# GpSimd forms u in 16 products of four channels a group instead of 8 of eight, with the decay slots turned from group to group, a loop of six groups and a reordered start

## The chip, the cores and the metric

The kernel runs on one core of a Trainium2 chip. The metric is the device time of one execution in microseconds (us); lower is better. The engines are TensorE (PE, its weight loads PEld), VectorE (DVE), ScalarE (ACT), GpSimd (POOL) and SyncE (SP), which issues the DMAs.

## The reference

The input has 128 sequences of 375 tokens with 64 channels (the tail that the means drop is not loaded: 372 are used). Three selective-scan layers follow one another, halving the length after the first two (372, 186, 93); then a diagonal state-space mixer and a routed small network, each added to its input. One scan layer is, cut to its core:

```
A = -exp(A_log)                                  # (64 channels e, 64 states n)
dlt, Bm, Cm = split(x @ W_dbc.T)                 # 1, 64 and 64 columns
delta = softplus(dlt * W_dt + b_dt)              # (b, l, 64)
dA = exp(delta[..., None] * A)
dBx = (delta * x)[..., None] * Bm[:, :, None, :]
h_t = dA_t * h_(t-1) + dBx_t                     # along l, for each channel and state
y = einsum('blen,bln->ble', h, Cm) + D * x       # then the mean of two neighbours
```

The mixer behind it is a linear recurrence with constant complex factors (tables of sines and cosines are made for it once), the network picks one of 32 experts by an argmax.

## The kernel before, in words

Two sequences are put side by side, one state of one of the two sequences on each of the 128 partitions. A group is 744 columns' worth of tokens for two halves: 372 columns a channel. There are 64 groups in layer 0, 32 in layer 1 and 16 in layer 2, 112 in all. A group has 64 channels, taken as 32 pairs; a pair is one scan of 2 x 372 = 744 columns.

For each pair four engines work in a chain. PE spreads delta over the states (`spread_delta`, L400, two matmuls) into one of three slots of PSUM. ACT takes the exponential with the factor A in place (`decay`, L706, two activations). DVE runs the recurrence (`scan`, L923) from the decay slot and from u, into hT. PE then contracts hT with C (`fill`, L418), and ACT reads that out (`read_z`, L715). The slot of pair p is `p % 3` in every group (`pair_slot`), so a group's pairs 0 and 1 take the slots of pairs 30 and 31 of the group before: 32 isn't a multiple of three, and `spread_delta` waits there for a scan that lies two back, and three back elsewhere.

u is delta times x times B. DVE forms dx = delta * x once a group (`times_x`, L934), SP stores it to HBM, and SP loads it back, each channel broadcast over 64 partitions, in 16 pieces of two pairs, each two DMAs (`broadcast`, L294). u has four buffers of four pairs each, two pieces in one. POOL multiplies a whole buffer in place by B (`inject`, L1122): 2976 columns, once both pieces are there. DVE waits for u once in four pairs. A piece is loaded again once the scans of its two pairs are over (`s_scan`).

In between the engines prepare the next group: PE the three products with x (`item`) and the sums of the softplus (`sum_delta`, `take_off`), ACT its functions and B and C (`take_B`, `take_C`), at fixed pair numbers in each engine's `body`. PE also has matmuls whose result is thrown away (`keep_busy`, L428), three each at pairs 1, 8, 16 and 24. Every engine's instruction order is written out by hand; nothing is scheduled. `layer_bodies` writes the first two and the last two groups of a layer out and runs the others in a loop of two groups.

Ahead of the first group, all constants are loaded before the first x (L247 to L255); PE and ACT wait for all eleven. The tables of the mixer (L960 to L1005 on DVE, a chain of small operations with a handoff each; L835 to L841 on ACT with two loads of a function table) stand behind the preparation of group 0 and ahead of its first scan.

Of the kernel before, what the change touches and what calls it, by code (L numbers as in the profile page):

```python
# [11 lines left out]
P = 128  # L12
# [8 lines left out]
EPT = D // TILES_G  # L21
SLOTS = 3
# [36 lines left out]
def tower(nc, io, hs, out_dram, n_batch):  # L59
# [13 lines left out]
    with ctx:  # L73
# [47 lines left out]
        s_const, s_cast, s_dout, s_zero = sem("constants_loaded"), sem("spread_cast"), sem("d_out_ready"), sem("zeros_set")  # L121
# [8 lines left out]
        s_bc = [sem(f"broadcast{i}_loaded") for i in range(RING)]  # L130
# [72 lines left out]
        N_CONST = 11  # L203

        def pair_slot(p):

            return db[p % SLOTS][:, BANK - W0:BANK + W0]

# [5 lines left out]
        def layer_bodies(eng, body):  # L214


            def group(l, g):
                n = groups[l]
                here = (l, g)
                if isinstance(g, int) and g < 2:  # L220
                    prev = (l, g - 1) if g else ((l - 1, groups[l - 1] - 1) if l else None)
                    before = (l - 1, groups[l - 1] - 2 + g) if l else None
                else:
                    prev, before = (l, g - 1), (l, g - 2)
                if isinstance(g, int) and g == n - 1:
                    after = (l + 1, 0) if l + 1 < LAYERS else None
                else:
                    after = (l, g + 1)
                return here, prev, before, after

            for l in range(LAYERS):
                n = groups[l]
                for g in range(2):
                    body(g % 2, *group(l, g))
                with eng.Fori(1, n // 2 - 1) as k:
                    for half in range(2):
                        body(half, *group(l, 2 * k + half))
                for g in range(n - 2, n):
                    body(g % 2, *group(l, g))
# [6 lines left out]
        def _(sp):  # L246
            for dst, src in ((wdt, io["wdt"]), (wB, io["wB"]), (wC, io["wC"]), (a_log, io["a_log"])):  # L247
                sp.dma_start(dst[:, :, :], src.rearrange("l p m -> p l m")).then_inc(s_const, 16)
            sp.dma_start(cols[:, :], io["cols"]).then_inc(s_const, 16)
            sp.dma_start(d_diag[:, :, :], io["d_diag"].rearrange("l p m -> p l m")).then_inc(s_const, 16)  # L250
            sp.dma_start(own[:, :], io["own"]).then_inc(s_const, 16)
            sp.dma_start(tmap[:, :], io["tmap"]).then_inc(s_const, 16)
            sp.dma_start(eye[:, :], io["ident"]).then_inc(s_const, 16)
            for i in range(2):
                sp.dma_start(hT[i][:, 0:EPT * P // 2], io["spread"][:, i * EPT * P // 2:(i + 1) * EPT * P // 2]).then_inc(s_const, 16)  # L255

# [66 lines left out]
            def body(half, here, prev, before, after):  # L323
# [21 lines left out]
            load_x(first, 0)  # L345
            sp.dma_start(s5c, io["s5c"]).then_inc(m_small, 16)
            sp.dma_start(times, io["times"]).then_inc(m_small, 16)
            store_dx(first, 0)
# [29 lines left out]
        def _(pe):  # L378
            pe.wait_ge(s_const, 16 * N_CONST)
            pe.wait_ge(s_cast, 1)  # L380
            pe.wait_ge(s_zero, 5)
            pe.wait_ge(s_dout, 1)
            pe.wait_ge(s_neg, 2)

            def spread_delta(at, buf, p):
# [10 lines left out]
                slot = pair_slot(p).rearrange("p (e s t) -> p e s t", e=2, t=T)  # L396
# [107 lines left out]
            def body(half, here, prev, before, after):  # L504
                for p in range(PAIRS):
                    spread_delta(here, half, p)
# [6 lines left out]
                    if p in (8, 16, 24) or p == 1 and prev:  # L513
                        keep_busy(here, half, -1 if p == 1 else q - 1)
# [12 lines left out]
            item(first, 0, 0)  # L527
            for i in range(3):
                sum_delta(first, i)
            take_off(first, 0)  # L530
            take_off(first, 1)
            item(first, 0, 1)
            item(first, 0, 2)
            layer_bodies(pe, body)
# [142 lines left out]
        def _(act):  # L677
# [3 lines left out]
            act.wait_ge(s_const, 16 * N_CONST)  # L681
            nc.scalar.activation(a_log[:, :, :], a_log[:, :, :], ACT.Exp).then_inc(s_aexp, 1)
            act.wait_ge(s_aexp, 1)
            nc.scalar.mul(a_neg[:, :, :], a_log[:, :, :], -1.0).then_inc(s_aneg, 1)
            for l in range(LAYERS):
                last = nc.scalar.mul(d_diag[:, l, :], d_diag[:, l, :], 0.5 if pair_mean[l] else 1.0)
            last.then_inc(s_dout, 1)
            nc.scalar.mul(neg_eye[:, :], eye[:, :], -1.0).then_inc(s_neg, 1)  # L688
            act.wait_ge(s_aneg, 1)
            act.wait_ge(s_zero, 5)  # L690

            def decay(at, p):
                l, g = at
                T = LENGTHS[l]
                slot = pair_slot(p)
# [34 lines left out]
            def take_B(at, buf):  # L730
                n = G(at)
                act.wait_ge(s_item, 3 * n + 2)
                if not known_below(n, 2):
                    act.wait_ge(s_u, PRODS * (n - 1))
# [53 lines left out]
            def body(half, here, prev, before, after):  # L788
                for p in range(PAIRS):
                    decay(here, p)  # L790
# [37 lines left out]
            high(first)  # L828
            middle(first)
            low(first)  # L830
            take_B(first, 0)
            take_C(first, 0, 0)
            take_C(first, 0, 1)
            act.wait_ge(m_small, 16 * N_SMALL)
            nc.scalar.activation(col[:, 0:1], s5c[:, 2:3], ACT.Exp).then_inc(m_acol, 1)  # L835
            act.wait_ge(m_tab, 1)
            nc.scalar.activation(col[:, 3:4], col[:, 1:2], ACT.Exp).then_inc(m_acol, 1)
# [5 lines left out]
                act_func_set_id=EXPS_ON_JOINT_TABLE))  # L843
            layer_bodies(act, body)
# [54 lines left out]
        def _(dve):  # L899
# [7 lines left out]
            dve.wait_ge(s_const, 16 * N_CONST)  # L907
            for i in range(2):
                src = hT[i][:, 0:EPT * P // 2].rearrange("p (r m) -> p r m", m=P)
                last = nc.vector.tensor_copy(spread[:, i * EPT // 2:(i + 1) * EPT // 2, :], src)  # L910
            last.then_inc(s_cast, 1)
            dve.wait_ge(s_cast, 1)

            def scan(at, p):
# [8 lines left out]
                nc.vector.tensor_tensor_scan(hT[q % 2][:, i * PAIR:(i + 1) * PAIR], pair_slot(p),  # L923
# [12 lines left out]
            def body(half, here, prev, before, after):  # L936
                for p in range(PAIRS):
                    scan(here, p)
                    if after and p == 9:
                        times_x(after, 1 - half)  # L940

            times_x((0, 0), 0)
# [35 lines left out]
            ts(red, red, PI_LO, -PI_LO, ALU.min, ALU.max).then_inc(m_tab, 1)  # L978

# [131 lines left out]
        def _(pool):  # L1111
            tt = nc.gpsimd.tensor_tensor

            def inject(at, buf, c):

                n = G(at)
                slot = c % RING
                pool.wait_ge(s_bc[slot], 32 * HALVES * (PRODS // RING * n + c // RING + 1))
                if c == 0:
                    pool.wait_ge(s_read, 3 * n + 2)  # L1120
                here = u[slot][:, :].rearrange("p (e t) -> p e t", t=W0)
                tt(here, here, Bt[buf][:, :].unsqueeze(1).broadcast_to([P, 2 * HALVES * CHUNK, W0]), ALU.mult).then_inc(s_u, 1)  # L1122

            def body(half, here, prev, before, after):
                for c in range(PRODS):
                    inject(here, half, c)
# [139 lines left out]
```

## Time and profile before

| | |
|---|---|
| median of 3 runs | 6324.4 us (6324.39 to 6329.62) |
| the profiled execution's own time | 6317.07 us |
| its span, first to last instruction | 6315.2 us |
| busy: DVE, POOL, PE, ACT | 95%, 93%, 79%, 79% |
| DMA: mean rate, share of the 16 engines | 247 GB/s, 76% |
| TensorE clock granted, mean | 0.905 of full |

The profile comes from one execution. The span is what the trace covers. Busy shares are means over stages with different limits; a group of instructions is given with its line in the kernel, its count and the mean time of one. A wait is given with what ended it. "issue" means that nothing the profile shows was waited for. Lines of the timeline give the start, the time taken by the merged instructions and, in brackets, the idle time ahead of them.

### The profile page before, as it was taken

How to read it: one execution, taken by the hardware profiler on the slowest of the kernel's cores; microseconds unless marked ns; L12 is line 12 of the kernel's file. 1: busy time of each engine (PE TensorE's matmuls, PEld its weight loads, DVE VectorE, ACT ScalarE, POOL GpSimd, SP SyncE). 2: the span in 40 equal slices, each digit the busy share in tenths (PEclk: the TensorE clock that was granted, in tenths of full speed). 3: DMA queues.
4: the chain of work that ended last, by engine and by line, in shares of the span. 5: the costliest groups of instructions: out<-in, count | busy, mean ns of one | idle time of the engine just before them, and what ended most of it. 6: DMA issues, size and time to landing. Idle time of an engine off the chain costs nothing.

```text
span 6315.2 us, 115575 instructions
## 1 busy us (share of the span) xinstructions
PE 4964.2 (79%) x35373; PEld 2008.5 (32%) x35373; DVE 6002.6 (95%) x4016; ACT 4959.9 (79%) x10247; POOL 5895.7 (93%) x996
## 2 busy tenths in 40 slices
PE   5777777777877777777787877778777778777789
PEld 2333333333333333333333333333333333333234
DVE  7999999999999999999999999999999999999965
ACT  5888888888888888888888877787887888887744
POOL 6999999999999999999999999999999999999933
PEclk7999999999899999999989888898998898998899
DMA  6887788787888888878888877788787787887810
GB/s 196 261 261 262 260 263 260 263 260 263 259 262 260 262 262 262 262 261 261 262 261 264 261 258 254 256 260 260 256 260 252 258 263 261 266 259 260 264 41 14
DMA packets 561605, 1561.17 MB, mean 247 GB/s; under 512 B 172113, under 2 KB 320530, under 8 KB 561298
## 3 DMA queue, kind: packets, MB, share of 16 engines
q1 hardware_dynamic: 561426, 1559.30, 76.0%
q8 instruction: 49, 0.80, 0.1%
q14 instruction: 130, 1.06, 0.0%
HBM read 1468.37 MB, written 90.59 MB: 247 GB/s over the span
## 4 chain that ended last, share of the span: by engine, by line
DVE 47%; issue 27%; PE 16%; POOL 4%; ACT 3%; DVEq 1%; DMA 1%; SPq 0%; ACTq 0%; POOLq 0%
DVE hT L923 46%; PE z_bank L418 5%; POOL u L1122 4%; PE decay L400 4%; ACT decay L706 2%; PE decay L540 2%; PE z_bank L428 1%; PE prep_bank L499 1%; DVEq L922 1%; PE decay L598 1%; DVE dx L934 1%; PE prep_bank L618 1%; PE prep_bank L444 1%; DMA u<-dx_rows 1%; PE decay L604 0%
## 5 line engine op out<-in xcount | busy, mean ns | idle before, releaser
L1122 POOL TENSOR_TENSOR u<-u,Bt 128x2976 f32<-128x2976 f32 x896 | 5788.6, 6495 | 219.0 <-DMA u<-dx_rows 217.3
L923 DVE TENSOR_TENSOR_SCAN hT<-decay,u 128x744 f32<-128x744 f32 x3584 | 5767.9, 1682 | 144.5 <-ACT decay L706 141.4
L706 ACT ACTIVATE decay<-decay,a_neg 128x371 f32<-128x371 f32 (+2 forms) x7168 | 3634.8, 555 | 641.1 <-PE decay L400 615.2
L400 PE MATMUL decay<-stk,spread 96*128 96x371 bf16 (+2 forms) x7168 | 1924.1, 356 | 1301.4 <-DVE hT L923 1206.3
L418 PE MATMUL z_bank<-hT,Cst 128*32 128x256 f32 x21472 | 1630.6, 427 | 0.0
L400 PEld LDWEIGHTS decay<-stk,spread 96*128 96x128 bf16 x7168 | 452.9, 101 | 2853.8 <-DVE hT L923 2616.7
L715 ACT COPY z_sb<-z_bank 128x512 f32<-128x512 f32 x1342 | 805.6, 600 | 375.3 <-PE z_bank L418 374.6
L418 PEld LDWEIGHTS z_bank<-hT,Cst 128*32 128x32 f32 x21472 | 601.4, 118 | 787.9 <-issue 545.0
L428 PE MATMUL z_bank<-stk,spread 96*128 96x372 bf16 x1341 | 325.5, 357 | 0.0
L499 PEld LDWEIGHTS prep_bank<-tmap,yT 64*128 64x128 f32 x1344 | 203.5, 215 | 134.5 <-issue 133.2
L499 PE MATMUL prep_bank<-tmap,yT 64*128 64x32 f32 (+3 forms) x1344 | 243.2, 306 | 0.7 <-DMA yT<-y_rows 0.7
L472 PE MATMUL prep_bank<-delta,eye 128*128 128x372 f32 x448 | 182.7, 489 | 2.2 <-DVE dx L934 1.7
L428 PEld LDWEIGHTS z_bank<-stk,spread 96*128 96x128 bf16 x1341 | 143.7, 107 | 106.0 <-issue 39.1
L444 PE MATMUL prep_bank<-xT,w_dt_rows 128*128 128x372 f32 x224 | 131.1, 678 | 16.1 <-ACT neg_eye L688 13.0
L1153 POOL TENSOR_TENSOR hT<-hT 128x372 f32<-128x372 f32 x16 | 15.5, 972 | 134.5 <-DVE hT L1038 134.5
L744 ACT ACTIVATE Cst<-prep_bank,own_batch 128x384 f32<-128x384 f32 x224 | 132.3, 591 | 1.7 <-PE prep_bank L444 1.7
L866 ACT ACTIVATE hT<-decay,u 128x372 f32<-128x372 f32 x64 | 36.5, 570 | 110.4 <-PE z_bank L604 110.4
L721 ACT ACTIVATE t_abs<-prep_bank,cols 128x372 f32<-128x372 f32 x112 | 74.3, 663 | 47.0 <-issue 24.7
L454 PE MATMUL prep_bank<-t_w,eye 128*128 128x372 f32 x224 | 98.3, 522 | 1.8 <-ACT t_w L753 1.8
L768 ACT COPY delta<-prep_bank 128x372 f32<-128x372 f32 x112 | 52.5, 469 | 57.0 <-PE prep_bank L462 56.6
L474 PE MATMUL prep_bank<-parts,neg_eye 128*128 128x372 bf16 x336 | 91.3, 326 | 0.0
L461 PE MATMUL prep_bank<-t_ln,eye 128*128 128x372 f32 x224 | 89.8, 482 | 0.0
(138 smaller groups left out, 2497.8 us busy)
## 6 DMA issues: line engine op xcount, KB each, us to landing
u<-dx_rows SPq DMA_DIRECT2D x3584, 372.0 KB, 4.1
delta_parts<-parts SPq DMA_DIRECT2D x112, 279.0 KB, 6.8
stk<-delta_parts SPq DMA_DIRECT2D x112, 279.0 KB, 5.3
y_rows<-z_sb SPq DMA_DIRECT2D x1792, 12.0 KB
yT<-y_rows SPq DMA_DIRECT2D x112, 192.0 KB, 4.4
dx_rows<-dx SPq DMA_DIRECT2D x112, 186.0 KB, 2.8
xT<-in_x SPq DMA_DIRECT2D x64, 186.0 KB, 4.3
xP<-in_x SPq DMA_DIRECT2D x64, 186.0 KB, 4.1
```

What stands on the lines that cost most here:

```text
L400: nc.tensor.matmul(slot[:, e, :, 1:], spread[0:PARTS * QR, TILES_G * q + er // TILES_G, :], src[:, er % TILES_G, :, 1:], start=True, stop= ...
L418: last = nc.tensor.matmul(bank[TB * 2 * g:TB * 2 * (g + 1), kk * EPT * TB:(kk + 1) * EPT * TB], Cst[buf][:, CG * (2 * i + kk) + g, :, :], ...
L428: nc.tensor.matmul(zb[:, 0:W0], spread[0:PARTS * QR, 0, :], stk[buf][0:PARTS * QR, 0, :], start=True, stop=True)
L444: nc.tensor.matmul(prep[:, 0:W0], (wdt, wB, wC)[i][:, l, :], xT[buf][:, :], start=True, stop=True).then_inc(s_item, 1)
L472: nc.tensor.matmul(prep[:, 0:W0], eye[:, :], delta[:, :], start=True, stop=False)
L499: last = nc.tensor.matmul(prep[:, k * w:k * w + m], yT[:, k, :], tmap[:, base:base + m], start=False, stop=(k == KB - 1))
L540: return nc.tensor.matmul(dst, wt, src, start=start, stop=stop)
L706: last = nc.scalar.activation(bank, bank, ACT.Exp, scale=a_neg[:, l, c:c + 1])
L715: nc.scalar.copy(z_sb[buf][:, 2 * i:2 * i + 2, :, q * EPT:(q + 1) * EPT], src).then_inc(s_zev, 1)
L744: ins = nc.scalar.activation(Cst[buf][:, :, b, :], prep[:, 0:COLS_Z].rearrange("p (k t) -> p k t", t=TB), ACT.Identity, scale=own[:, b:b + 1])
L923: nc.vector.tensor_tensor_scan(hT[q % 2][:, i * PAIR:(i + 1) * PAIR], pair_slot(p), u[c % RING][:, part * PAIR:(part + 1) * PAIR], 0.0, AL ...
L1122: tt(here, here, Bt[buf][:, :].unsqueeze(1).broadcast_to([P, 2 * HALVES * CHUNK, W0]), ALU.mult).then_inc(s_u, 1)
```

## The change

- u: `inject` is called 16 times a group, each with one piece (two pairs, four channels, 1488 columns), and waits for that piece alone; there are eight semaphores for the pieces instead of four, and `scan` waits for u once in two pairs.
- Slots: `pair_slot(turn, p)` goes on from group to group, so that each pair waits for the scan three before it.
- Loop: since the slots come round after three groups and the two sets of buffers after two, the loop holds six groups (`ROUND_OF_GROUPS`).
- Idle-filling matmuls: `keep_busy` at pair 25 too, and `keep_busy_in_prep`, three more at pair 31.
- Start: the inputs of the tables and of the first product are loaded first and have a semaphore of their own; DVE makes the tables' first half before anything else, and ACT's functions of A follow behind the first B.

```diff
+ROUND_OF_GROUPS = 6
-        def pair_slot(p):
+        def pair_slot(turn, p):
 
-            return db[p % SLOTS][:, BANK - W0:BANK + W0]
+            return db[(turn + p) % SLOTS][:, BANK - W0:BANK + W0]
...
+            def turn(l, g):
+                return PAIRS * (gbase[l] + g) % SLOTS
+
             for l in range(LAYERS):
                 n = groups[l]
-                for g in range(2):
-                    body(g % 2, *group(l, g))
-                with eng.Fori(1, n // 2 - 1) as k:
-                    for half in range(2):
-                        body(half, *group(l, 2 * k + half))
+
+                first = 2 + (n - 4) % ROUND_OF_GROUPS
+                for g in range(first):
+                    body(g % 2, turn(l, g), *group(l, g))
+                with eng.Fori(0, (n - 2 - first) // ROUND_OF_GROUPS) as k:
+                    for g in range(ROUND_OF_GROUPS):
+                        body(g % 2, turn(l, first + g), *group(l, ROUND_OF_GROUPS * k + (first + g)))
...
# broadcast
-                    sp.dma_start(dst, src).then_inc(s_bc[prod % RING], 16)
+                    sp.dma_start(dst, src).then_inc(s_bc[c % (RING * HALVES)], 16)
...
# SP, the start
+            sp.dma_start(s5c, io["s5c"]).then_inc(m_small, 16)
+            sp.dma_start(times, io["times"]).then_inc(m_small, 16)
+            load_x(first, 0)
+            sp.dma_start(wdt[:, :, :], io["wdt"].rearrange("l p m -> p l m")).then_inc(s_first, 16)
+            sp.dma_start(cols[:, :], io["cols"]).then_inc(s_first, 16)
+            sp.dma_start(eye[:, :], io["ident"]).then_inc(s_first, 16)
...
# spread_delta
-                if p >= SLOTS:
+                if p >= SLOTS or not known_below(n, 1):
                     pe.wait_ge(s_scan, PAIRS * n + p - SLOTS + 1)
-                elif not known_below(n, 1):
-                    pe.wait_ge(s_scan, PAIRS * n - (2, 1, 3)[p] + 1)
...
+            def keep_busy_in_prep(at, buf, before):
+
+                pe.wait_ge(s_post, G(before) + 1)
+                for _ in range(3):
+                    nc.tensor.matmul(prep[:, 0:W0], spread[0:PARTS * QR, 0, :], stk[buf][0:PARTS * QR, 0, :],
+                                     start=True, stop=True)
...
-                    if p in (8, 16, 24) or p == 1 and prev:
+                    if p in (8, 16, 24, 25) or p == 1 and prev:
                         keep_busy(here, half, -1 if p == 1 else q - 1)
...
+                    if prev and p == 31:
+                        keep_busy_in_prep(here, half, prev)
...
# scan
-                if part == 0:
-                    dve.wait_ge(s_u, PRODS * n + c + 1)
+                if part % CHUNK == 0:
+                    dve.wait_ge(s_u, CHUNKS * n + p // CHUNK + 1)
...
# inject
-                slot = c % RING
-                pool.wait_ge(s_bc[slot], 32 * HALVES * (PRODS // RING * n + c // RING + 1))
+                slot = c % (RING * HALVES)
+                pool.wait_ge(s_bc[slot], 32 * (CHUNKS // (RING * HALVES) * n + c // (RING * HALVES) + 1))
...
-                here = u[slot][:, :].rearrange("p (e t) -> p e t", t=W0)
-                tt(here, here, Bt[buf][:, :].unsqueeze(1).broadcast_to([P, 2 * HALVES * CHUNK, W0]), ALU.mult).then_inc(s_u, 1)
+                half = u[slot // HALVES][:, slot % HALVES * CHUNK * PAIR:(slot % HALVES + 1) * CHUNK * PAIR]
+                here = half.rearrange("p (e t) -> p e t", t=W0)
+                tt(here, here, Bt[buf][:, :].unsqueeze(1).broadcast_to([P, 2 * CHUNK, W0]), ALU.mult).then_inc(s_u, 1)
```

In the instruction order of the built programs this stands as follows. POOL's first products of group 0, before:

```order
L1122 TENSOR_TENSOR u<-u,Bt 128x2976 [waits item_read,broadcast0_loaded]
L1122 TENSOR_TENSOR u<-u,Bt 128x2976 [waits broadcast1_loaded]
L1122 TENSOR_TENSOR u<-u,Bt 128x2976 [waits broadcast2_loaded]
L1122 TENSOR_TENSOR u<-u,Bt 128x2976 [waits broadcast3_loaded]
L1122 TENSOR_TENSOR u<-u,Bt 128x2976 [waits broadcast0_loaded]
```

and the same channels in the changed program (each `broadcastN_loaded` is one piece, where it was two):

```order
L1138 TENSOR_TENSOR u<-u,Bt 128x1488 [waits item_read,broadcast0_loaded]
L1138 TENSOR_TENSOR u<-u,Bt 128x1488 [waits broadcast1_loaded]
L1138 TENSOR_TENSOR u<-u,Bt 128x1488 [waits broadcast2_loaded]
L1138 TENSOR_TENSOR u<-u,Bt 128x1488 [waits broadcast3_loaded]
L1138 TENSOR_TENSOR u<-u,Bt 128x1488 [waits broadcast4_loaded]
L1138 TENSOR_TENSOR u<-u,Bt 128x1488 [waits broadcast5_loaded]
L1138 TENSOR_TENSOR u<-u,Bt 128x1488 [waits broadcast6_loaded]
L1138 TENSOR_TENSOR u<-u,Bt 128x1488 [waits broadcast7_loaded]
L1138 TENSOR_TENSOR u<-u,Bt 128x1488 [waits broadcast0_loaded]
```

Twice as many instructions, each of half the columns and with one wait.

PE at pairs 24 to 26 of a group (L400 is a pair's two matmuls, L428 the idle-filling ones), before:

```order
L400 MATMUL decay<-stk,spread 128x371
L428 MATMUL z_bank<-stk,spread 128x372 [waits z_read]
L428 MATMUL z_bank<-stk,spread 128x372 x2
L400 MATMUL decay<-stk,spread 128x371 [waits scan_done]
L400 MATMUL decay<-stk,spread 128x371
L400 MATMUL decay<-stk,spread 128x371 [waits scan_done]
L400 MATMUL decay<-stk,spread 128x371
```

and in the changed program:

```order
L400 MATMUL decay<-stk,spread 128x371
L428 MATMUL z_bank<-stk,spread 128x372 [waits z_read]
L428 MATMUL z_bank<-stk,spread 128x372 x2
L400 MATMUL decay<-stk,spread 128x371 [waits scan_done]
L400 MATMUL decay<-stk,spread 128x371
L428 MATMUL z_bank<-stk,spread 128x372 [waits z_read]
L428 MATMUL z_bank<-stk,spread 128x372 x2
L400 MATMUL decay<-stk,spread 128x371 [waits scan_done]
L400 MATMUL decay<-stk,spread 128x371
```

Three matmuls stand between pair 25 and pair 26 that did not.

DVE ahead of the first dx (`z_sb` holds the tables' operands here), before:

```order
L906 MEMSET hT 128x16 x2
L910 CAST spread<-hT 128x1024 [waits constants_loaded]
L910 CAST spread<-hT 128x1024
L934 TENSOR_TENSOR dx<-prep_bank,xT 128x372 [waits x_loaded,delta_hi,spread_cast]
L960 TENSOR_TENSOR z_sb<-z_sb 128x1 [waits m_cols_exp,m_small_loaded]
```

and in the changed program, the end of the chain and what follows it:

```order
L975 SCALAR_TENSOR_TENSOR z_sb<-z_sb 128x93 [waits m_dve_chain]
L983 SCALAR_TENSOR_TENSOR z_sb<-z_sb 128x93 [waits m_dve_chain]
L984 TENSOR_SCALAR z_sb<-z_sb 128x93 [waits m_dve_chain]
L989 CAST spread<-hT 128x1024 [waits constants_loaded]
L989 CAST spread<-hT 128x1024
L941 TENSOR_TENSOR dx<-prep_bank,xT 128x372 [waits x_loaded,delta_hi,spread_cast]
L996 TENSOR_TENSOR tables<-z_sb 128x93 [waits m_sins]
```

The first half of the chain has moved ahead of the casts and of dx; its second half still stands between dx and the first scan.

## Rows read from the trace of the kernel before

**Rows 1.** Scans and products by line: durations in ns, first and last start.

```profile
L923 DVE TENSOR_TENSOR_SCAN hT<-decay,u x3584: 1673/1680/1708, 67.4 to 6017.8; 128x744 f32<-128x744 f32 x200
...
L1122 POOL TENSOR_TENSOR u<-u,Bt x896: 6450/6493/6554, 35.2 to 6001.5; 128x2976 f32<-128x2976 f32 x180
```

**Rows 2.** Timeline, DVE and POOL in layer 0: start, us, instructions.

```profile
84.56 25.67 DVE L923 TENSOR_TENSOR_SCAN hT<-decay,u 128x744 f32<-128x744 f32 x16 [0.36 <-ACT decay L706]
...
2253.35 0.52 DVE L934 TENSOR_TENSOR dx<-prep_bank,xT 128x372 f32<-128x372 f32 x1
2253.79 40.18 DVE L923 TENSOR_TENSOR_SCAN hT<-decay,u 128x744 f32<-128x744 f32 x25
...
2271.16 51.64 POOL L1122 TENSOR_TENSOR u<-u,Bt 128x2976 f32<-128x2976 f32 x8 [2.18 <-DMA u<-dx_rows]
```

**Rows 3.** Stretches of the three layers, L923 alone: length, busy (count), clock, DMA.

```profile
300.00:3300.00 3000.00, 2920.58 (x1815) 0.91 0.80 261
3660.00:5000.00 1340.00, 1280.48 (x797) 0.89 0.79 257
5380.00:5900.00 520.00, 502.52 (x313) 0.91 0.81 261
```

**Rows 4.** Who waited for whom: us in total, times, longest.

```profile
POOL u L1122 <- DMA u<-dx_rows: 217.3, 180, 34.8
...
DVE hT L923 <- ACT decay L706: 141.4, 180, 2.4
...
ACT t_abs L721 <- issue: 24.7, 13, 2.5
```

**Rows 5.** Timeline of a group boundary in layer 0, PE and DVE.

```profile
1229.40 0.49 PE L400 MATMUL decay<-stk,spread 96*128 96x371 bf16 x2 [2.71 <-DVE hT L923]
...
1233.27 1.94 PE L418 MATMUL z_bank<-hT,Cst 128*32 128x256 f32 x16
...
1236.80 6.50 DVE L923 TENSOR_TENSOR_SCAN hT<-decay,u 128x744 f32<-128x744 f32 x4 [0.94 <-ACT decay L706]
...
1239.07 1.07 PE L418 MATMUL z_bank<-hT,Cst 128*32 128x256 f32 x16
```

**Rows 6.** Timeline behind the loop's branch in layer 1, ACT and DVE.

```profile
3775.41 0.66 ACT L721 ACTIVATE t_abs<-prep_bank,cols 128x372 f32<-128x372 f32 x1 [2.06 <-issue]
...
3776.99 14.49 DVE L923 TENSOR_TENSOR_SCAN hT<-decay,u 128x744 f32<-128x744 f32 x9 [1.90 <-ACT decay L706]
```

**Rows 7.** Timeline of the start, all engines.

```profile
13.01 1.58 PE L444 MATMUL prep_bank<-xT,w_dt_rows 128*128 128x372 f32 x2 [13.01 <-ACT neg_eye L688]
...
25.91 1.13 SPq L294 DMA_DIRECT2D u<-dx_rows  x2
...
29.87 0.47 ACT L735 COPY Bt<-prep_bank 128x372 f32<-128x372 f32 x1 [1.70 <-PE prep_bank L444]
...
35.19 0.21 DVE L965 TENSOR_SCALAR z_sb<-z_sb 128x93 f32<-128x93 f32 x1
35.23 25.72 POOL L1122 TENSOR_TENSOR u<-u,Bt 128x2976 f32<-128x2976 f32 x4 [34.78 <-DMA u<-dx_rows]
35.43 6.34 DVE L966 TENSOR_SCALAR z_sb<-z_sb 128x93 f32<-128x93 f32 x1
...
38.79 0.80 PE L400 MATMUL decay<-stk,spread 96*128 96x371 bf16 x2 [6.79 <-DMA stk<-delta_parts]
...
67.37 16.08 DVE L923 TENSOR_TENSOR_SCAN hT<-decay,u 128x744 f32<-128x744 f32 x10
```

**Rows 8.** POOL's products of 372 columns in the mixer, by line.

```profile
L1153 POOL TENSOR_TENSOR hT<-hT x16: 969/972/975, 6034.9 to 6270.4; 128x372 f32<-128x372 f32 x16
...
L1138 POOL TENSOR_TENSOR u<-hT,tables x16: 1444/1448/1452, 6037.7 to 6274.2; 128x372 f32<-128x372 f32 x16
...
L1144 POOL TENSOR_TENSOR u<-u x16: 1267/1276/1283, 6040.3 to 6276.8; 128x372 f32<-128x372 f32 x16
```

**Rows 9.** The broadcasts' DMA issues: count, size, median us to landing.

```profile
u<-dx_rows SPq DMA_DIRECT2D x3584, 372.0 KB, 4.1
```

More of the change, by code:

```diff
@@ L246, in _ @@
         def _(sp):
[L247 to L255, printed above, removed]
             def load_x(at, buf):
@@ L321, in store_h, with body @@
                 sp.dma_start(hs[l][:, bass.ds(g * n, n)], y_out[:, 0:n]).then_inc(s_store, 16)
-            def body(half, here, prev, before, after):
+            def body(half, turn, here, prev, before, after):
                 for c in range(CHUNKS):
@@ L502, in to_channels, with body @@
                     last.then_inc(s_Y, 1)
-            def body(half, here, prev, before, after):
+            def body(half, turn, here, prev, before, after):
                 for p in range(PAIRS):
-                    spread_delta(here, half, p)
+                    spread_delta(here, half, turn, p)
                     q, i = divmod(p, TPAIRS)
@@ L680, in _, with decay @@
                 act_func_set_id=EXPS_ON_JOINT_TABLE))
[L681 to L687, printed above, removed]
+            act.wait_ge(m_small, 16 * N_SMALL)
+            nc.scalar.activation(col[:, 0:1], s5c[:, 2:3], ACT.Exp).then_inc(m_acol, 1)
+            act.wait_ge(m_tab, 1)
+            nc.scalar.activation(col[:, 3:4], col[:, 1:2], ACT.Exp).then_inc(m_acol, 1)
+            act.wait_ge(s_first, 16 * N_FIRST)
             nc.scalar.mul(neg_eye[:, :], eye[:, :], -1.0).then_inc(s_neg, 1)
-            act.wait_ge(s_aneg, 1)
             act.wait_ge(s_zero, 5)
-            def decay(at, p):
+            def decay(at, turn, p):
                 l, g = at
                 T = LENGTHS[l]
-                slot = pair_slot(p)
+                slot = pair_slot(turn, p)
                 act.wait_ge(s_arg, D * G(at) + 2 * p + 1)
@@ L786, in post, with body @@
                 nc.scalar.copy(y_out[:, 0:w], prep[:, 0:w]).then_inc(s_post, 1)
-            def body(half, here, prev, before, after):
+            def body(half, turn, here, prev, before, after):
                 for p in range(PAIRS):
-                    decay(here, p)
+                    decay(here, turn, p)
                     q, i = divmod(p, TPAIRS)
@@ L827, in _ @@
             logarithm(first)
[L828 to L837, printed above, removed]
             act.wait_ge(m_tab, 2)
@@ L843, in _ @@
                 act_func_set_id=EXPS_ON_JOINT_TABLE))
+            high(first)
+            middle(first)
+            low(first)
+            act.wait_ge(s_const, 16 * N_CONST)
+            take_B(first, 0)
+            nc.scalar.activation(a_log[:, :, :], a_log[:, :, :], ACT.Exp).then_inc(s_aexp, 1)
+            act.wait_ge(s_aexp, 1)
+            nc.scalar.mul(a_neg[:, :, :], a_log[:, :, :], -1.0).then_inc(s_aneg, 1)
+            for l in range(LAYERS):
+                last = nc.scalar.mul(d_diag[:, l, :], d_diag[:, l, :], 0.5 if pair_mean[l] else 1.0)
+            last.then_inc(s_dout, 1)
+            take_C(first, 0, 0)
+            take_C(first, 0, 1)
+            act.wait_ge(s_aneg, 1)
             layer_bodies(act, body)
@@ L906, in _, with scan @@
                 nc.vector.memset(h[:, EPT * W0:EPT * W0 + TB], 0.0).then_inc(s_zero, 1)
[L907 to L914, printed above, removed]
+            def scan(at, turn, p):
                 n = G(at)
@@ L934, in times_x, with body @@
                 tt(dx[:, :], prep[:, 0:W0], xT[buf][:, :], ALU.mult).then_inc(s_dx, 1)
-            def body(half, here, prev, before, after):
+            def body(half, turn, here, prev, before, after):
                 for p in range(PAIRS):
-                    scan(here, p)
+                    scan(here, turn, p)
                     if after and p == 9:
                         times_x(after, 1 - half)
-            times_x((0, 0), 0)
             dve.wait_ge(m_small, 16 * N_SMALL)
@@ L978, in _ @@
             ts(red, red, PI_LO, -PI_LO, ALU.min, ALU.max).then_inc(m_tab, 1)
+            dve.wait_ge(s_const, 16 * N_CONST)
+            for i in range(2):
+                src = hT[i][:, 0:EPT * P // 2].rearrange("p (r m) -> p r m", m=P)
+                last = nc.vector.tensor_copy(spread[:, i * EPT // 2:(i + 1) * EPT // 2, :], src)
+            last.then_inc(s_cast, 1)
+            dve.wait_ge(s_cast, 1)
+            times_x((0, 0), 0)
             dve.wait_ge(m_abig, 2)
```

36 lines of the change are left out of this document (21 added, 15 removed).

## The prediction

> **What bounds the kernel now.** The page comes first. Its shares of busy time name two engines, DVE and POOL, and its groups name one line on each: 3584 scans (L923) and 896 products (L1122). Next those two lines by themselves: the scans start from 67.4 to 6017.8, the products from 35.2 to 6001.5 [rows 1]. So 112 groups take 5952 us, 53.1 each, ahead of them stands a start of 67.4, and behind the last scan's start a tail of 6315.2 - 6017.8 = 297.4. The three are priced apart.
>
> Inside a group, scans in a row start (25.67 - 1.68) / 15 = 1.60 apart, and the dx product takes the DVE for 2253.79 - 2253.35 = 0.44 [rows 2]. A group without a wait is 32 x 1.60 + 0.44 = 51.6. The counts by stage give 3000 / (1815 / 32) = 52.9 in layer 0, 53.8 in layer 1, 53.2 in layer 2 [rows 3]. So 1.3, 2.2 and 1.6 a group are lost, and the chain of waits says to what: "ACT decay" 141.4 over the kernel, and no row has the DVE waiting for POOL's u; POOL waits 217.3 in all for the broadcasts [rows 4]. It runs eight products in 51.64 [rows 2] and then waits for a buffer, so it works at the pace of the scans with some 1.3 us a group to spare. That spare time is what this change spends.
>
> Where the DVE loses its time is seen in one boundary of layer 0 [rows 5]. PE waits 2.71 for a scan, since pair 0 and pair 1 of a group go into the slots of pairs 30 and 31 of the one before, two scans back instead of three. The matmuls behind that idle time run at the lower of PE's two clocks (1.2 instead of 2.4 GHz): a fill (L418) takes 1.94, the same sixteen matmuls 1.07 a few us later. ACT gets pair 3 late, and the DVE stands 0.94. In layer 1 something else joins it once in two groups: ACT sits 2.06 with "issue" just behind the loop's branch, and the DVE stands 1.90 [rows 6]; such stops come 13 times and take 24.7 in all [rows 4].
>
> **The start.** Four tiny DVE operations of the S5 tables take 6.4 each, because a POOL product runs beside them; one of the same shape just ahead of POOL's first product takes 0.21 [rows 7]. They hold the first scan until 67.37, although its matmuls ran at 38.79. In the new order this chain stands ahead of everything; its inputs are the first two DMAs. Some twenty operations of 0.2 and their handoffs are 4 to 5 us, so it is over by 11, and nothing that PE needs waits for it. PE's first matmul waits for six early loads instead of eleven and the casts; these are issued by about 4 and with at most the 4.1 to landing of the large broadcasts [rows 9] for the x among them, the second or third to be issued, they are there by 6.5: PE starts near 6.5 instead of 13.01, so 6.5 us gained. Sin with its two table loads stands in ACT behind the logarithm, where ACT waits for PE's sum of delta anyway. The rest of the chain moves with PE: first decay matmuls 38.79 - 6.5 = 32.3. The two matmuls (0.80), a copy and two exps (0.555 each in the page's group) and three handoffs between engines are some 2.7, so I put the first scan at 35, 32 us earlier. POOL needs one broadcast half and Bt instead of both halves: Bt is copied at 29.87, which becomes 23.9 with its 0.47, and the first half is issued at 25.91 - 6.5 = 19.4 in two DMAs over 1.1 us and lands 4.1 after the second [rows 7, 9]. POOL starts at 25, 10 earlier. Bounds for the first scan: 33 (all moves by 6.5 and a little more) to 42 (nothing but the tables leaves).
>
> **The slots, the new idle-filling matmuls, the loop.** With the turn each pair waits for the scan three before it, across the boundary too. PE has 1.6 more at pairs 0 and 1, and three matmuls are added at pair 25 and three at pair 31: 3 x 0.33 = 1 us of PE, or 0.63 at the upper level, in the stretch where it stands idle before the boundary's 2.71; they cost nothing while it idles. The wait on y_out at pair 31 was met one pair before, when ACT copied it. Of 1.3 us a group I leave 0.3, for ACT's extra operations around the boundary; bounds 0 and the present 1.3.
>
> The loop body goes from two groups to six. The stop behind the branch [rows 6] is the price: 16 turns and three exits at 2.0 each are 38 us on the DVE's path, against 25 now. The Trainium skill (Runtime: NRT & Kernel Launch, Instruction fetch mechanics) says that an engine holds 512 instructions, TensorE 2048, and that a taken branch to a page outside stalls; a six-group body passes both, so by it every turn of every layer stops, on ACT and PE. The stop of 2.06 in layer 1 agrees, and no row shows one on PE.
>
> So the DVE's own path puts the last scan at 35 + 112 x 51.64 - 1.6 + 34 + 38 = 5889, 129 earlier than now.
>
> **The products.** 896 of 2976 columns become 1792 of 1488. The element work stays; each product's fixed part is paid twice. No row has 1488 columns; the nearest plain ones have 372 and take 0.972 [rows 8], against 6.493 for 2976 [rows 1]. The slope is 5.521 / 2604 = 2.12 ns a column, the fixed part 0.184, so a product of 1488 is 3.337. Starts in a row are (51.64 - 6.49) / 7 = 6.45 apart, 0.04 under the duration [rows 2], which leaves 3.29 from start to start, 52.7 a group instead of 51.6. Lower bound: if all of the fixed part lies under the product ahead, 3.225 and 51.6 again. Upper bounds: other rows of 372 columns take 1.276 and, with a repeated table, 1.448 [rows 8], giving 3.47 and 3.57 by the same line, 55.5 and 57.1 a group. I take the row of 0.972. L1144 has the same plain operands and takes 1.276 all the same, with DVE work on the same tiles beside it, so it is that company which costs there; a scan beside a product costs it nothing (25.72 for four ahead of the scans is 6.42 a start [rows 7], 6.45 among them).
>
> The Trainium skill (GPSIMD Engine Reference, Elementwise — side-by-side cycle accounting) reports 4.497 us for a tensor_tensor of 2048 fp32 columns on GpSimd. An estimate from it and the 6.493 here has a slope of 2.15 and a fixed part of only 0.09, which is 3.25 from start to start and 52.0 a group; that is the first rival's case below, and no run here has 2048 columns.
>
> At 52.7 POOL is slower than the DVE's 51.6 + 0.3 + 0.3 = 52.2, and it becomes the bound: the scans, always waiting for ACT, wait for a product instead. Its head start of 10 us lasts for some 20 groups. What the finer grain gives back is small then: a product needs one half instead of two, so the ring's room grows (from a half freed to its next use are 14 scans, 22.4 us, less 1.2 of issue, 4.1 to landing [rows 9] and 3.3 of product: 13.8 instead of 7.3), and POOL's waits [rows 4] should go nearly to zero. Stops of 2 us in ACT or PE are caught up inside that room.
>
> **The sum.** POOL starts at 25, 1792 x 3.29 = 5896 later it is done, at 5921. The last two scans start 0.1 and 1.7 behind it: 5922.5 instead of 6017.8. The tail's code and waits are unchanged, 297.4. Span 6220. The profiled execution stands 1.9 over its span and the median of the three runs 7.3 over that: 6229, 95 less than 6324.4. The 1.1 a group of the split costs 34 us against what the rest alone would give (6196).
>
> **Rivals.**
> - *The DVE stays the bound* (0.22). The fixed part is hidden, a group of products is under 52.2, and the time is the DVE's path: 5889 + 297.4 + 9.2 = 6196. For it: starts are closer than durations. Against: the row of 372 columns is 0.18 above its share of columns.
> - *The fixed part is larger and the split eats all* (0.09). POOL at 3.47 would end at 25 + 6218 = 6243, and the time is 6243 + 1.7 + 297.4 + 9.2 = 6552. The point from which the change is slower is (6324.4 - 9.2 - 297.4 - 1.7 - 25) / 1792 = 3.343 from start to start, only 0.05 above my value; the two dearer rows of 372 columns speak for it [rows 8], the plain one against.
> - *Code fetch costs more than the ring can hold* (0.10). Six groups are three times the code: if PE, ACT and SP each stop at a turn, one behind the other, 6 us, and the room of 13.8 is cut by SP's late broadcasts, some 2 of these reach POOL at each of 19 places, to which the DVE adds none: 6229 + 38 = 6267.
> - *POOL the bound as forecast*: 0.59. Its own range, 3.26 to 3.32, is 6175 to 6283.
>
> Three runs of this kernel can tell 0.2% (13 us) from no change. Faster by more: the forecast, the first and the third rival, 0.91, of which I leave 0.02 for the third grown to no change. Slower 0.09, same 0.02, faster 0.89. The range 6172 to 6295 leaves out the second rival and the far ends of the others.
>
> **What would show it.** First scan near 35, first product near 25; a product of 3.34 us, starts 3.29 apart and eight in a row without a wait; the DVE's waits named POOL u and not ACT decay, about 1 us a group; PE's wait at the boundary no longer 2.7, and fills near 1.07 there; some 2 us stops of ACT once in six groups; last scan near 5922; tail 297. The prediction is wrong if the product is over 3.38 or under 3.28, if the DVE still waits for ACT in most groups, or if the first scan is later than 42.

## The result and the profile after

The changed kernel takes 6236.05 us (median of 4 runs, 6232.0 to 6237.6); the kernel before, with a run more beside it, 6324.4 (6320.94 to 6329.62). The ratio is 0.9859, interval 0.9842 to 0.9876: 88 us faster. The forecast was 6229, with a range of 6172 to 6295. The profiled execution took 6232.0 us, its span is 6229.2. Its page (busy time, chain of waits, costliest groups, DMA queues of instructions):

```profile
PE 4777.0 (77%) x36042; PEld 1973.4 (32%) x36042; DVE 5999.1 (96%) x4016; ACT 5014.3 (80%) x10247; POOL 6013.7 (97%) x1892
...
q8 instruction: 325, 5.32, 0.4%
q14 instruction: 374, 3.06, 0.1%
...
POOL 76%; issue 11%; DVE 6%; PE 6%; DMA 1%; ACT 1%; SPq 1%; DVEq 0%; ACTq 0%; POOLq 0%
...
L1138 POOL TENSOR_TENSOR u<-u,Bt 128x1488 f32<-128x1488 f32 x1792 | 5906.6, 3328 | 23.4 <-DMA u<-dx_rows 23.4
L930 DVE TENSOR_TENSOR_SCAN hT<-decay,u 128x744 f32<-128x744 f32 x3584 | 5788.4, 1682 | 84.9 <-ACT decay L716 79.0
```

The chain of work that ended last is now 76% POOL; it was 47% DVE and 4% POOL. The one idle time of L1138 is that ahead of its first product, so POOL never waits again. Instruction transfers on q8 went from 49 packets (0.80 MB) to 325 (5.32 MB); no engine but PE, with its 36042 matmuls and as many weight loads, executes enough instructions to need that much, so q8 is taken for PE's. The same lines by themselves, against [rows 1] (ns; first and last start in us):

```profile
L1138 POOL TENSOR_TENSOR u<-u,Bt x1792: 3305/3328/3356, 23.8 to 5927.1; 128x1488 f32<-128x1488 f32 x200
...
L930 DVE TENSOR_TENSOR_SCAN hT<-decay,u x3584: 1676/1677/1709, 33.1 to 5932.3; 128x744 f32<-128x744 f32 x200
```

(5927.1 - 23.8) / 1791 = 3.296 from start to start, over the whole kernel. First scan 33.1 instead of 67.4, last scan 5932.3 instead of 6017.8, tail 296.9 instead of 297.4: of the 86 us of span, 34 come from the start and 51 from the groups between the scans. The start, against [rows 7]:

```profile
5.61 1.61 PE L451 MATMUL prep_bank<-xT,w_dt_rows 128*128 128x372 f32 x2 [5.61 <-DMA eye<-in_ident]
...
7.14 0.21 DVE L984 TENSOR_SCALAR z_sb<-z_sb 128x93 f32<-128x93 f32 x1
...
20.41 0.47 ACT L745 COPY Bt<-prep_bank 128x372 f32<-128x372 f32 x1 [1.10 <-PE prep_bank L451]
...
23.84 22.98 POOL L1138 TENSOR_TENSOR u<-u,Bt 128x1488 f32<-128x1488 f32 x7 [23.38 <-DMA u<-dx_rows]
30.95 0.14 PEld L400 LDWEIGHTS decay<-stk,spread 96*128 96x128 bf16 x2 [9.73 <-issue]
30.99 0.78 PE L400 MATMUL decay<-stk,spread 96*128 96x371 bf16 x2 [9.16 <-DMA stk<-delta_parts]
...
33.08 1.71 DVE L930 TENSOR_TENSOR_SCAN hT<-decay,u 128x744 f32<-128x744 f32 x1 [12.02 <-ACT decay L716]
```

The operations that took 6.34 now take 0.2 to 0.3, with no product beside them: POOL's first starts at 23.84. A group boundary in layer 0 that is no turn of the loop, against [rows 5]:

```profile
1238.02 0.49 PE L400 MATMUL decay<-stk,spread 96*128 96x371 bf16 x2 [0.64 <-DVE hT L930]
...
1239.62 0.49 PE L400 MATMUL decay<-stk,spread 96*128 96x371 bf16 x2 [0.48 <-DVE hT L930]
...
1241.64 1.07 PE L418 MATMUL z_bank<-hT,Cst 128*32 128x256 f32 x16
```

PE waits 0.64 where it waited 2.71, and the fill takes 1.07 where it took 1.94: the boundary looks like any other place. But one boundary in six is a turn of the loop, where PE branches back to the start of the body, and there stands what was not before:

```profile
445.56 0.63 PE L435 MATMUL prep_bank<-stk,spread 96*128 96x372 bf16 x3
...
451.65 0.80 PE L400 MATMUL decay<-stk,spread 96*128 96x371 bf16 x2 [5.46 <-issue]
...
452.18 1.00 ACT L716 ACTIVATE decay<-decay,a_neg 128x371 f32<-128x371 f32 x2 [5.50 <-PE decay L400]
...
453.22 1.71 DVE L930 TENSOR_TENSOR_SCAN hT<-decay,u 128x744 f32<-128x744 f32 x1 [3.25 <-ACT decay L716]
```

PE sits 5.46 with "issue" behind the branch and the DVE loses 3.25, then 0.39 and 0.90 more before the row of pairs is full again, 4.5 in all. The waits give it 13 times:

```profile
PE decay L400 <- issue: 67.6, 13, 6.3
...
DVE hT L930 <- POOL u L1138: 3.2, 1, 3.2
```

Thirteen is the number of branches that are taken. The three layers go through their loops 10, 4 and 2 times, 16 passes (the "turns" of the expectations), and PE branches back 9 + 3 + 1 = 13 times; behind the last pass of a layer no stop of PE is listed.

The layers' stretches, L930 alone, against [rows 3]:

```profile
300.00:3300.00 3000.00, 2934.86 (x1823) 0.97 0.81 264
3600.00:4900.00 1300.00, 1275.73 (x789) 0.97 0.82 263
5300.00:5850.00 550.00, 540.08 (x334) 0.97 0.82 265
```

That is 52.7, 52.7 and 52.7 a group, where it was 52.9, 53.8 and 53.2, and the granted clock 0.97 instead of 0.91, 0.89 and 0.91. Three layers with one period, and it is 16 x 3.296.

### The profile page after: what moved, and what is told of

It reads as the page before. It is cut to its first block, busy times and chain, and to the rows that moved or that the text cites. A ratio compares the mean times of both kernels' runs of the same rounds, so it can differ in the third digit from the quotient of the medians.

```text
span 6229.2 us, 117436 instructions
## 1 busy us (share of the span) xinstructions
PE 4777.0 (77%) x36042; PEld 1973.4 (32%) x36042; DVE 5999.1 (96%) x4016; ACT 5014.3 (80%) x10247; POOL 6013.7 (97%) x1892
## 3 DMA queue, kind: packets, MB, share of 16 engines
q8 instruction: 325, 5.32, 0.4%
## 4 chain that ended last, share of the span: by engine, by line
POOL 76%; issue 11%; DVE 6%; PE 6%; DMA 1%; ACT 1%; SPq 1%; DVEq 0%; ACTq 0%; POOLq 0%
POOL u L1138 76%; DVE hT L930 5%; PE decay L553 2%; PE decay L611 1%; PE prep_bank L631 1%; PE z_bank L418 1%; ACT decay L716 0%; DMA u<-dx_rows 0%; PE decay L400 0%; SPq L299 0%; PE decay L617 0%; SPq L290 0%; DMA z_sb<-h_after 0%; PE prep_bank L553 0%; DMA y_rows<-z_sb 0%
## 5 line engine op out<-in xcount | busy, mean ns | idle before, releaser
L1138 POOL TENSOR_TENSOR u<-u,Bt 128x1488 f32<-128x1488 f32 x1792 | 5906.6, 3328 | 23.4 <-DMA u<-dx_rows 23.4
L930 DVE TENSOR_TENSOR_SCAN hT<-decay,u 128x744 f32<-128x744 f32 x3584 | 5788.4, 1682 | 84.9 <-ACT decay L716 79.0
L400 PE MATMUL decay<-stk,spread 96*128 96x371 bf16 (+2 forms) x7168 | 1808.5, 336 | 1404.6 <-DVE hT L930 1233.0
L418 PE MATMUL z_bank<-hT,Cst 128*32 128x256 f32 x21472 | 1492.2, 396 | 2.0 <-issue 1.7
L400 PEld LDWEIGHTS decay<-stk,spread 96*128 96x128 bf16 x7168 | 422.8, 98 | 2905.9 <-DVE hT L930 2728.9
L418 PEld LDWEIGHTS z_bank<-hT,Cst 128*32 128x32 f32 x21472 | 573.4, 111 | 693.2 <-issue 467.4
L428 PE MATMUL z_bank<-stk,spread 96*128 96x372 bf16 x1677 | 362.2, 325 | 0.0
L506 PE MATMUL prep_bank<-tmap,yT 64*128 64x32 f32 (+3 forms) x1344 | 219.8, 285 | 0.0
L428 PEld LDWEIGHTS z_bank<-stk,spread 96*128 96x128 bf16 x1677 | 165.4, 99 | 107.2 <-issue 7.2
L451 PE MATMUL prep_bank<-xT,w_dt_rows 128*128 128x372 f32 x224 | 100.1, 531 | 13.6 <-DMA xT<-in_x 6.6
L464 PE MATMUL prep_bank<-t_one,eye 128*128 128x372 f32 x224 | 89.6, 481 | 0.0
```

The lines of the kernel that those rows point to most:

```text
L400: nc.tensor.matmul(slot[:, e, :, 1:], spread[0:PARTS * QR, TILES_G * q + er // TILES_G, :], src[:, er % TILES_G, :, 1:], start=True, stop= ...
L418: last = nc.tensor.matmul(bank[TB * 2 * g:TB * 2 * (g + 1), kk * EPT * TB:(kk + 1) * EPT * TB], Cst[buf][:, CG * (2 * i + kk) + g, :, :], ...
L451: nc.tensor.matmul(prep[:, 0:W0], (wdt, wB, wC)[i][:, l, :], xT[buf][:, :], start=True, stop=True).then_inc(s_item, 1)
L506: last = nc.tensor.matmul(prep[:, k * w:k * w + m], yT[:, k, :], tmap[:, base:base + m], start=False, stop=(k == KB - 1))
```

## The experiments

Ratios are to the kernel before, measured beside each; the before medians of the three sessions were 6317.6, 6323.0 and 6315.5. All ratios have intervals of 0.001 to 0.004 to either side. Where two runs of different sessions are compared, the difference of medians is given and, where it says something else, that of the ratios times 6320.

| run | products | slots turned | filling at 25, 31 | groups in the loop, branches taken | median us | ratio |
|---|---|---|---|---|---|---|
| changed kernel | 16 | yes | yes | 6, 13 | 6236.05 | 0.9859 |
| e1_eight | 8 | yes | yes | 6, 13 | 6186.31 | 0.9797 |
| e4_thirtytwo | 32 | yes | yes | 6, 13 | 6487.80 | 1.0267 |
| e6_loop12 | 16 | yes | yes | 12, 5 | 6234.67 | 0.9864 |
| e7_no_fill | 16 | yes | no | 6, 13 | 6248.50 | 0.9891 |
| e5_eight_loop12 | 8 | yes | yes | 12, 5 | 6148.44 | 0.9728 |
| e9_eight_loop30 | 8 | yes | yes | 30, 1 | 6127.59 | 0.9698 |
| e8_eight_no_fill | 8 | yes | no | 6, 13 | 6260.47 | 0.9903 |
| e10_fill_only | 8 | no | yes | 2, 47 | 6259.05 | 0.9914 |
| e3_start_only | 8 | no | no | 2, 47 | 6285.14 | 0.9949 |
| e2_split_only (old start) | 16 | no | no | 2, 47 | 6313.75 | 0.9992 |

**The split undone.** The changed kernel with whole buffers as products:

```diff
-                slot = c % (RING * HALVES)
-                pool.wait_ge(s_bc[slot], 32 * (CHUNKS // (RING * HALVES) * n + c // (RING * HALVES) + 1))
+                slot = c % RING
+                pool.wait_ge(s_bc[slot], 32 * HALVES * (PRODS // RING * n + c // RING + 1))
...
-                for c in range(CHUNKS):
+                for c in range(PRODS):
```

> The changed kernel with 8 products of eight channels again; slots, loop of six, filling matmuls and start as changed. Theory P (POOL's products alone set the changed kernel's time, 1792 starts 3.297 apart without a wait): with 6.45 a product POOL would be done by 23.8 + 5779 = 5803, so the DVE's own path decides: first scan 33.1, 112 x 51.64, and 16 turns of the loop at about 4.8 (a PE stop of 5.5 behind the branch, of which the DVE loses 3.25 + 0.39 + 0.90): last scan near 5900, time near 6205, 30 less than the changed kernel. Rival D (the DVE's path with its turns sets the time already and POOL is merely busy): no change, 6236 within 5. A third: the finer products also help, by their earlier waits, so that going back costs: over 6240.

Measured 6186.3: 50 faster than the changed kernel by the medians, 39 by the ratios, 49 by the start of the last scan (6205 was expected). Products and scans by line:

```profile
L1137 POOL TENSOR_TENSOR u<-u,Bt x896: 6446/6499/6672, 28.0 to 5868.7; 128x2976 f32<-128x2976 f32 x180
...
L930 DVE TENSOR_TENSOR_SCAN hT<-decay,u x3584: 1676/1677/1708, 34.5 to 5883.3; 128x744 f32<-128x744 f32 x200
```

POOL waits for broadcasts again (90.3 us in 57 places, 27.5 of them ahead of its first product), so it isn't the bound, and the last scan starts at 5883.3. Rival D and the third fall. It is 19 under what was expected, and most of that is the count of the stops: 16 were priced at 4.8, PE stops at the 13 branches taken, and 3 x 4.8 = 14.

**The split alone, in the kernel before** (its edits put into the old kernel):

> The kernel before with nothing but the 16 products of four channels. Theory P: 16 x 3.297 = 52.75 a group is still under the 53.1 at which the scans go there, so POOL only loses its waits for broadcasts: 6324 within 10, POOL's waits down from 217 to under 40. Rival (the fixed part is paid on the path wherever it stands): 112 x 1.2 = 134 more, 6458. Rival (the finer grain lets the scans start earlier): under 6310.

Measured 0.9992, interval 0.9982 to 1.0002, no change. POOL's waits fall from 217.3 (34.8 of them ahead of the first product) to 58.3 for broadcasts, where under 40 was expected, and 31.2 ahead of the first product. The fixed part costs nothing as long as the scans need 53.1 a group, and the finer grain brings nothing either: apart from one wait of 0.5 no scan waited for u there, and none in the kernel before.

**The start alone:**

> The reordered start alone: slots p % 3, loop of two groups, no added filling matmuls, 8 products. Theory: the first scan comes at 33 instead of 67.4 and nothing else moves: 6324 - 34 = 6290. Rival (POOL's lead from the long start was worth something, so part is given back): 6300 to 6320. A group stays 52.9 in layer 0.

Measured 6285.1, 32 under the before of its session (34 expected): the first scan stands at 33.3 and the last at 5980.9, 5947.6 between them against 5950.4. That POOL's lead over the scans is shorter costs nothing.

**The products cut once more:**

```diff
-                tt(here, here, Bt[buf][:, :].unsqueeze(1).broadcast_to([P, 2 * CHUNK, W0]), ALU.mult).then_inc(s_u, 1)
+                for k in range(2):
+                    two = here[:, CHUNK * k:CHUNK * (k + 1), :]
+                    tt(two, two, Bt[buf][:, :].unsqueeze(1).broadcast_to([P, CHUNK, W0]), ALU.mult).then_inc(s_u, 1)
```

> The changed kernel with each product cut once more: 32 products of 744 columns a group. Theory P with a fixed part per product: 6.450 for 2976 and 3.297 for 1488 give 2.119 ns a column and 0.144 fixed, so 1.720 from start to start, 55.05 a group; last product at 23.8 + 3584 x 1.720 = 6188, time 6188 + 1.7 + 297 + 7 = 6494. Rival D: POOL not the bound, so less than that: 6236 plus only what exceeds the scans' 52.6, about 6440 at most with its start-up lead. If the fixed part is hidden under the product ahead: 6236.

Measured 6487.8 (6494 forecast):

```profile
L1140 POOL TENSOR_TENSOR u<-u,Bt x3584: 1738/1764/1887, 23.4 to 6182.7; 128x744 f32<-128x744 f32 x200
```

(6182.7 - 23.4) / 3583 = 1.719 from start to start. So 744, 1488 and 2976 columns take 1.719, 3.296 and 6.45 (the last from eight in a row, [rows 2]): 2.12 ns a column and 0.14 fixed, a straight line through three sizes. The durations (1.764, 3.328, 6.493) have the same slope and a fixed part of 0.18, so 0.04 of it lies under the product ahead and 0.14 does not.

**The length of the loop, with 8 products and with 16** (`ROUND_OF_GROUPS = 12`; in the run of thirty the loop is left out where no groups remain for it):

> 8 products and a loop of twelve groups instead of six, so 8 turns instead of 16, all else as changed. Theory (where the DVE is the bound, each turn costs it the PE stop behind the branch, 4 to 5 us): 8 x 4.8 = 38 less than the run with 8 products and a loop of six, near 6167. Rival (the stop is taken out of waits that would come anyway): no difference to that run.

> The changed kernel (16 products) with a loop of twelve groups, 8 turns instead of 16. Theory P: POOL never waits, a PE stop is caught up in the ring of u, so no change: 6236 within 4. Rival D: 8 x 4.8 = 38 less, 6198.

> 8 products and a loop of thirty groups: 2 turns in layer 0, the groups of the other layers written out. By 4.8 a turn it should be 6 x 4.8 = 29 under the loop of twelve (ratio to before 0.9728, 6148): near 6120. The floor of both engines is 33 + 112 x 51.64 + 297 + 4 = 6118, so no less than that. Rival (streaming three times the code costs the loads of u something, or the residual waits are not the turns'): 6140 and over.

The branches taken are 13, 5 and 1 with loops of six, twelve and thirty groups, and PE's listed stops with 8 products are just as many: 13 with 71.7 us, 5 with 27.0, 1 with 6.0. Eight stops fewer save 37.9 (4.7 each; 38 expected), four fewer again 20.9 (5.2 each, across sessions; 29 expected, for six turns). The runs of six and thirty differ by 58.7 in 12 stops, 4.9 each. With 16 products the step from six to twelve saves 1.4, nothing that can be told. That is the clearest pair: the stops cost in the one case and not in the other. Why is seen in the rows of scans of e6_loop12 in layer 0, two groups ahead of a stop and one behind it:

```profile
572.62 52.40 DVE L930 TENSOR_TENSOR_SCAN hT<-decay,u 128x744 f32<-128x744 f32 x32
...
678.12 52.38 DVE L930 TENSOR_TENSOR_SCAN hT<-decay,u 128x744 f32<-128x744 f32 x32
...
770.79 4.90 DVE L930 TENSOR_TENSOR_SCAN hT<-decay,u 128x744 f32<-128x744 f32 x3 [4.01 <-ACT decay L716]
...
788.52 51.23 DVE L930 TENSOR_TENSOR_SCAN hT<-decay,u 128x744 f32<-128x744 f32 x32
```

Held by POOL, 32 scans take 52.40 (52.75 from group to group, POOL's 16 products); behind a stop they take their own 51.23, so the DVE wins back 1.2 a group until the stop is made up. In the run of thirty with 8 products, scans by line and the DVE's waits are:

```profile
L931 DVE TENSOR_TENSOR_SCAN hT<-decay,u x3584: 1676/1677/1707, 34.5 to 5824.4; 128x744 f32<-128x744 f32 x200
...
  ACT decay L717: 12.8, 11
```

(5824.4 - 34.5 + 1.6) / 112 = 51.7 a group, the DVE's own 51.6. 6120 was expected and over 6140 by the rival. This is the fastest version found, 6127.6 us, 0.9698 (0.9665 to 0.9731): 108 under the changed kernel by the medians, 102 by the ratios.

**The filling matmuls, and the slots, apart:**

> The changed kernel without the filling matmuls at pairs 25 and 31. Theory P: the granted clock falls from 0.97 towards 0.90 and the DVE waits more for ACT, but POOL still sets the time: 6236 within 5. Rival (the clock carries part of the gain): up to 1 us a group, 6280 to 6340.

> 8 products, and without the filling matmuls at pairs 25 and 31. Here the DVE is the bound, so what the clock is worth must show: with fills of 1.94 instead of 1.07 behind a boundary the DVE should lose some 0.3 to 0.9 a group, 34 to 100 more than the run with 8 products that has them. If the turned slots alone had cured the boundary: no difference to that run.

> 8 products, the new start, the filling matmuls at pairs 25 and 31, but slots p % 3 and the loop of two groups (no PE stops behind the branch). Theory (the boundary's loss is both the slot's shorter reach and PE's lower clock): filling alone cures a part, between the start-only run (6285, 0.9949) and the run with turned slots and eight products without its turns (about 6186 - 77 = 6110): 6180 to 6240. Rival (the clock is all of it): 6135 or less. Rival (the slots are all of it): 6280.

With 16 products, taking the filling away costs 12 by the medians and 20 by the ratios (0.9891 against 0.9859), over the 5 that I allowed; against e6_loop12, of the same session, it is 14. The products there:

```profile
L1136 POOL TENSOR_TENSOR u<-u,Bt x1792: 3304/3341/3493, 23.6 to 5936.7; 128x1488 f32<-128x1488 f32 x200
...
  DMA u<-dx_rows: 9.5, 17
```

POOL waits 17 times for 9.5: the scans fell so far behind that the ring of u ran out, and it ends 9.6 later. So POOL's rate is a bound only while the scans keep up within the ring. Here they hardly do: the DVE waits for ACT 117 times (129.4), and the time is within the noise of the run with 8 products and no filling (0.9891 and 0.9903), which speaks for the DVE's own path as the limit of most of it; it was not tested apart. With 8 products taking the filling away costs 74 (67 by the ratios; 34 to 100 expected). What each part is worth is best read from one stretch of layer 0, the scans alone, in the runs e3, e10, e8 and e1 in this order (neither, filling, slots, both):

```profile
700.00:3250.00 2550.00, 2482.06 (x1544) 0.91 0.81 261
```

```profile
700.00:3250.00 2550.00, 2486.26 (x1547) 0.93 0.80 262
```

```profile
700.00:3250.00 2550.00, 2466.87 (x1537) 0.91 0.81 262
```

```profile
700.00:3250.00 2550.00, 2496.82 (x1560) 0.98 0.82 265
```

These are 52.85, 52.75, 53.09 and 52.31 a group. The last two hold PE's stop in every sixth group, eight times in this stretch; the run of thirty has one there and 51.71 a group, so a stop is worth 4.2 here (0.6 x 48.75 groups / 7), eight of them 0.7 a group, and without them the two are 52.4 and 51.6. Filling alone gives 0.1, the slots alone some 0.5, both 1.2. I had put filling alone at 6180 to 6240 and it came at 6259. The granted clock goes with it: 0.93 with the filling alone, 0.91 with the slots alone, 0.98 with both. The rows show that the lower level stands in two places. With filling but the slots of before (e10), PE is still idle 2.23 at the boundary, and the fill behind it takes 1.93:

```profile
1197.05 0.49 PE L402 MATMUL decay<-stk,spread 96*128 96x371 bf16 x2 [2.23 <-DVE hT L932]
...
1200.93 1.93 PE L420 MATMUL z_bank<-hT,Cst 128*32 128x256 f32 x16
...
1204.46 11.29 DVE L932 TENSOR_TENSOR_SCAN hT<-decay,u 128x744 f32<-128x744 f32 x7 [0.94 <-ACT decay L718]
```

With the slots turned but no filling (e8), the level falls in some groups ahead of the boundary, at the last pairs, and the DVE stands 0.65:

```profile
1238.78 1.94 PE L418 MATMUL z_bank<-hT,Cst 128*32 128x256 f32 x16
...
1246.63 3.33 DVE L928 TENSOR_TENSOR_SCAN hT<-decay,u 128x744 f32<-128x744 f32 x2 [0.65 <-ACT decay L714]
```

Of some 577 fills of sixteen matmuls in the stretch, those over 1.5 us are 80 with neither edit, 54 with the filling, 98 with the slots and 13 with both. So each of the two edits alone leaves one of the places. Which of the two filling places does it was not tried.

## Why the prediction was right

- *The start*: first scan 33.1 (35 forecast), POOL 23.8 (25), PE's first matmul 5.61 (6.5). The run with it alone gives 32 us, as forecast.
- *POOL becomes the bound at 3.29 a product*: 3.296 measured, no wait after the first; confirmed from three sides, by e1 (fewer, larger products are 39 to 50 faster), e4 (smaller ones cost what the line says) and e6 (fewer turns bring nothing). POOL was to be done at 5921 and is at 5930. The span is 9 over the sum for it; the median stands 6.9 over the span and not 9.2, which leaves 7 in the time. How close the two paths lie is seen at the stops: six groups take POOL 316.4, and the DVE's own 6 x 51.64 with a stop of 4.5 is 314.4.
- *The lower fixed part of the first rival*: no. The estimate of 3.25 that goes with the Trainium skill (GPSIMD Engine Reference, Elementwise — side-by-side cycle accounting) is 0.046 low; the measured three sizes decide. With it POOL's end would have been 82 us earlier and the DVE's path the bound.
- *The DVE's own path*, put at 5889: e1 shows it at 5883.3. But its terms were not right one by one. I gave 0.3 a group to ACT's operations at the boundary, 34 us; e9 shows under 0.1. I gave 38 us to turns, as 2 us stops of ACT in 19 places (16 turns and three exits); they are PE's stops at 13 branches, 5.2 on average, which cost the DVE 4.9 each, 64 us. The two errors nearly cancel, and that the path came out is luck.
- *The place of the stop*: the prediction had only ACT's stop in its rows and said so. In the changed kernel ACT's ("t_abs <- issue", 24.7 before) is not among the waits, and PE's is; since ACT waits 5.50 for PE there, a shorter stop of its own would not be seen. The Trainium skill (Runtime: NRT & Kernel Launch, Instruction fetch mechanics) has the rule by which it would be PE: TensorE holds 2048 instructions, and a taken branch to a place outside what is held stalls. The traces agree in that q8 has 49 packets and PE no such stop with loops of two groups, 325 packets and stops of some 5 us with that of six. The trace has 312 matmuls and as many weight loads a group in layer 0 (17764 of each in 1823 / 32 groups), so 3700 for six groups and, with 306 of each before, 1200 for two: the one is past the 2048 of the Trainium skill and the other is not, counting these instructions alone.
- *What the split costs*: forecast 34 against the rest alone; measured 39 to 50: the rest alone is at 6186 and not 6196, and POOL ended 9 later than forecast.
- *The signs*: two were wrong. The stops once in six groups are not ACT's of 2 us but PE's. And I expected the DVE's waits to name POOL, about 1 us a group; only one of 3.2 does. The DVE's idle time is put down to ACT (48 waits, 79.0, of which 12.0 stand ahead of the first scan and most of the rest at the stops). Behind a stop the DVE is late and runs some four groups at its own 51.23 for 32 scans; only then is it held for POOL, by tenths that stay under what the view lists, here 51.94:

```profile
1205.91 51.23 DVE L930 TENSOR_TENSOR_SCAN hT<-decay,u 128x744 f32<-128x744 f32 x32
1257.06 0.52 DVE L941 TENSOR_TENSOR dx<-prep_bank,xT 128x372 f32<-128x372 f32 x1
1257.50 51.94 DVE L930 TENSOR_TENSOR_SCAN hT<-decay,u 128x744 f32<-128x744 f32 x32
```

So "the scans wait for a product instead" held for a part of the groups only. Who the bound is was seen in POOL's own row (no idle time at all) and in the chain, not in the DVE's waits. The third rival's size of fetch stops (6 us) was about right, its path to POOL was not: none reached it.

## What to carry to other kernels

Cutting work on an engine with slack is free until its fixed part times the count fills the slack; then it is paid in full, so the count has to be weighed against the pace that the other edits of the same change leave (53.1 before, 51.6 after: the split cost nothing in the first and 39 to 50 us in the second). An engine that never waits from its first to its last instruction is the bound, whatever the others' waits are named after. And where a loop is unrolled to make a rotation come round, price its branch, by the times that it is taken, on each engine and above all on the one with the most instructions: here, once the bound was off POOL, fewer and longer turns were worth 59 us more.

## What the runs showed of the hardware that I had not expected

- A loop body of six groups stops PE 5.2 us on average behind its branch (13 times, 67.6 us in all, up to 6.3), one of two groups doesn't stop it. The stops are as many as the branches taken (13, 5 and 1 with 8 products), and each cost 4.2 to 4.9 us of time where the DVE was the bound.
- Filling an engine's idle time and shortening it were worth 0.1 and 0.5 us a group one by one and 1.2 together, with granted clocks of 0.93, 0.91 and 0.98 against 0.91; alone, each leaves one of the two places where PE falls to its lower level.
- GpSimd products of 744, 1488 and 2976 columns lie on one line: 2.12 ns a column and 0.14 us each, start to start; of the 0.18 that the durations have, 0.04 is hidden.
